# Statistics, routing lists and late weights of an eight-core attention and expert layer in another order

## The reference

```python
x = x + attn(layernorm(x))          # Q = ln @ Wq + bq; K = V = Q
#   probs = softmax(Q @ Q.T / 32);  out = probs @ Q        (2048 x 1024 a core)
x = x + ffn(layernorm(x))
#   scores = sigmoid(h @ gate_w.T);  top 4 of 32 experts by scores + e_bias
#   weights = chosen scores / their sum
#   out = sum over chosen e of  weight_e * (silu(h @ w1[e]) * (h @ w3[e])) @ w2[e]
#   w1, w3: 1024 x 768, w2: 768 x 1024, float32
```

## Time and profile before

| | |
|---|---|
| median of three runs | 1770.35 us (1752.7 to 1800.26) |
| the profiled execution | 1748.2 us; its span 1746.8 us, so 1.4 us lie outside |
| cores in it | 1707.2 to 1746.8 us; the page is of the slowest |
| busy share of the span | PE 72%, PEld 40%, ACT 25%, DVE 23%, POOL 21% |
| granted clock of PE, mean | 0.856 on that core |
| HBM, that core | 349.21 MB read, 52.72 MB written |
| Q phase, attention phase, expert phase | 0 to 124, 124 to 480, 480 to 1747 us |

### The profile page before, as it was taken

How to read it: one execution, slowest core, us unless ns; L and a number is a source line. 1 busy time by engine, 2 the same in 40 slices (tenths; PEclk the granted TensorE clock), 3 DMA queues, 4 the chain that set the end, 5 groups by cost and what they waited for, 6 DMA issues and landing times.

```text
span 1746.8 us, 20430 instructions; the slowest of 8 cores (1707.2 to 1746.8 us)
## 1 busy us (share of the span) xinstructions
PE 1250.8 (72%) x7138; PEld 705.6 (40%) x7209; DVE 399.3 (23%) x874; ACT 431.4 (25%) x613; POOL 367.4 (21%) x359
## 2 busy tenths in 40 slices
PE   4788987999606966666776776667677766677696
PEld 2444543555403533333343443344344433434353
DVE  3433543455501211111111111111111111111121
ACT  3443332333202211112222221122222211222131
POOL 0000011112322222222222222232222222322122
PEclk9889998999757988888888888888888887888898
DMA  9980265421167999999999999999999999999833
GB/s 203 194 167 13 73 62 47 58 78 62 50 71 127 168 169 171 171 169 170 171 169 167 165 166 167 169 167 161 173 169 175 173 167 168 170 164 166 160 70 55
DMA packets 45895, 241.72 MB, mean 138 GB/s; under 512 B 10424, under 2 KB 11064, under 8 KB 33248
## 3 DMA queue, kind: packets, MB, share of 16 engines
q0 software_dynamic: 35136, 209.95, 72.7%
q1 hardware_dynamic: 10512, 30.41, 8.0%
q10 hardware_dynamic: 144, 0.03, 0.0%
HBM read 349.21 MB, written 52.72 MB: 230 GB/s over the span
## 4 chain that ended last, share of the span: by engine, by line
DMA 54%; PE 27%; issue 9%; POOL 3%; DVE 2%; ACT 2%; POOLq 1%; DVEq 0%; SPq 0%; ACTq 0%
DMA out<-yb,t_meta 51%; PE pav L458 7%; PE pss L418 6%; PE pss L767 5%; POOL out L822 3%; PE ptr L296 2%; PE pav L798 2%; PE pss L340 2%; PE ptr L508 2%; DMA xg<-xnd,t_meta 2%; DMA xb<-xd 1%; DVE t_st L246 1%; DVE t_st L247 1%; ACT lnf L317 1%; DVE vq L347 0%
## 5 line engine op out<-in xcount | busy, mean ns | idle before, releaser
L296 PE MATMUL ptr<-c_idb,xg 128*128 128x128 bf16 x768 | 87.2, 297 | 380.4 <-DMA xg<-xnd,t_meta 366.1
L767 PE MATMUL pss<-xgt,wp 128*128 128x384 bf16 x2016 | 339.2, 328 | 1.4 <-ACT xgt L754 1.4
L767 PEld LDWEIGHTS pss<-xgt,wp 128*128 128x128 bf16 x2016 | 198.0, 98 | 135.9 <-issue 4.7
L296 PEld LDWEIGHTS ptr<-c_idb,xg 128*128 128x128 bf16 x768 | 72.9, 135 | 398.2 <-issue 397.8
L781 DVE TENSOR_TENSOR at<-sil,pss 128x384 bf16<-128x384 bf16 x192 | 106.5, 554 | 484.9 <-PE pss L767 484.9
L822 POOL DMA_INDIRECT out<-yb,t_meta x96 | 146.6, 1527 | 307.4 <-DMA out<-yb,t_meta 241.8
L807 DVE TENSOR_SCALAR yb<-pav,t_meta 128x512 f32<-128x512 f32 x96 | 72.1, 751 | 581.7 <-PE pav L798 576.8
L754 ACT COPY xgt<-ptr 128x1024 bf16<-128x1024 bf16 x96 | 97.2, 1012 | 433.5 <-PE ptr L296 353.8
L778 ACT ACTIVATE sil<-pss 128x384 bf16<-128x384 f32 x192 | 94.3, 491 | 358.4 <-PE pss L767 358.4
L767 PE MATMUL pss<-xgt,wr 128*128 128x384 bf16 x1056 | 178.8, 326 | 0.0
L798 PE MATMUL pav<-wp,at 128*128 128x512 bf16 x735 | 174.0, 396 | 4.1 <-issue 3.3
(11 more groups left out here) (100 smaller groups left out, 772.0 us busy)
## 6 DMA issues: line engine op xcount, KB each, us to landing
wp<-w1d POOLq DMA_DIRECT2D x21, 1536.0 KB, 40.6
wp<-w3d POOLq DMA_DIRECT2D x21, 1536.0 KB, 36.2
wp<-w2d POOLq DMA_DIRECT2D x21, 1536.0 KB, 29.5
wr<-w3d POOLq DMA_DIRECT2D x11, 1536.0 KB, 36.8
wr<-w2d POOLq DMA_DIRECT2D x11, 1536.0 KB, 31.1
wr<-w1d POOLq DMA_DIRECT2D x11, 1536.0 KB, 40.9
xb<-xd SPq DMA_DIRECT2D x32, 512.0 KB, 6.4
out<-xb SPq DMA_DIRECT2D x16, 512.0 KB, 3.5
```

The source lines that it names most:

```text
L296: ins = e.transpose(dst[:, k * 128:(k + 1) * 128], src_of(k), ident)
L767: ins = e.matmul(pss[:, bnk * 512:bnk * 512 + CAP], unit_ap(u, c * ID + ic * 128, 128), xgt[:, xo + c * CAP:xo + (c + 1) * CAP], start=(c ...
```

## The change

- The Q phase: `a_stats` only makes statistics; normalizing a tile is `a_ln`, one tile an iteration. The statistics of tiles `j + 3` and `j + 4` stand ahead of the bias add of tile `j` (odd `j`). The loads of x tiles 2 and 3 wait for the two halves of Wq. Of the weight units, one is issued for three tiles instead of one for two, so four in the loop, and the last three wait for the product of tile 12.
- Weights lie in memory in six pieces, each 128 rows x 1024 values (4 KB a row), 512 KB in one piece. A unit's DMA has 768 pieces of 4 KB to read and 2 KB to write where it had 128 of 24 and 12 KB.
- Units 7 to 10: `convert_unit` has POOL's queue round them from memory to memory (`wcd`) at the end of the Q phase and in the first three attention iterations. After attention SP loads the rounded copies, all four, 12 KB a row.
- Routing: tiles 14 and 15 are groups of their own. A record's row is place x 32 + expert, computed in float (the count is scaled by 32 as ACT copies it), neighbouring places 256 bytes apart; the list is read back in three runs of 256 bytes for each partition. Fewer DVE steps (two instructions instead of four in a Newton step; shift and mean folded into one), the mask first, the weights while PE counts; two small products of the combine weights go to POOL. The steps stand at fixed points, no longer 11 at a time.

The core of the diff:

```diff
+CONV = tuple(range(NP_UNITS, RING))
+PIECE = 1024
...
+GROUPS = [(j, j + 1) for j in range(0, NT - 2, 2)] + [(NT - 2,), (NT - 1,)]
...
-    w1d = nc.dram_tensor("w1d", [E, 128, UNIT], F32, kind="ExternalInput").ap()
...
+    w1d = nc.dram_tensor("w1d", [E, NPC, 128, PIECE], F32, kind="ExternalInput").ap()
...
-    mtd = nc.dram_tensor("mtd", [128 * 512, 2], U32, kind="Internal").ap()
+    wcd = nc.dram_tensor("wcd", [len(CONV), 128, UNIT], BF16, kind="Internal").ap()
+    mtd = nc.dram_tensor("mtd", [T * E, 2], U32, kind="Internal").ap()
...
-        for j in range(1, XR):
-            x_tok[j] = load_x(j)
+        x_tok[1] = load_x(1)
         t_bq = p.d(lambda e: e.dma_start(out=bq[:, :], in_=bqd), "dB")
-
-        mtv = mtd.rearrange("(q c) w -> q c w", q=128)
+        for j in range(2, XR):
+            x_tok[j] = load_x(j, t_wq[j - 2])
+
+        mtv = mtd[0:CAP * E, :].rearrange("(b q e) w -> q b (e w)", b=NB, q=128)
...
 
+        def convert_unit(k, *waits):
+
+            e_i, i = divmod(CONV[k], 3)
+            p.d(lambda e: e.dma_start(out=wcd[k, :, :].rearrange("p (c n) -> p c n", n=PIECE),
+                                      in_=wsrc[i][e_i, :, :, :].rearrange("c p n -> p c n")),
+                "dV", *waits, eng="gpsimd")
+
         def load_unit(u, *waits):
+            if u in CONV:
+                k = CONV.index(u)
+                u_tok[u] = p.d(lambda e: e.dma_start(out=unit_ap(u, 0, UNIT), in_=wcd[k, :, :]),
+                               f"dH{k}", p.cnt("dV"), *waits)
+                return
             e_i, i = divmod(u, 3)
-            u_tok[u] = p.d(lambda e: e.dma_start(out=unit_ap(u, 0, UNIT),
-                                                 in_=wsrc[i][e_i, :, :]),
+            u_tok[u] = p.d(lambda e: e.dma_start(
+                out=unit_ap(u, 0, UNIT).rearrange("p (c n) -> p c n", n=PIECE),
+                in_=wsrc[i][e_i, :, :, :].rearrange("c p n -> p c n")),
                            f"dU{u % RING}", *waits, eng="gpsimd")
 
...
             for j in tiles:
-                s = j % XR
-                ln_tok[j] = p.s(lambda e, j=j, s=s: e.activation(
-                    lnf[:, (j % 2) * H:(j % 2 + 1) * H], xb[:, s * H:(s + 1) * H],
-                    AF.Identity, bias=col(C_NMR + j), scale=col(C_RSTD + j)),
-                    v_r, tl_tok.get(j - 2))
-                if j + XR < NT:
-                    x_tok[j + XR] = load_x(j + XR, ln_tok[j])
-                    if j % 2 == 0:
-                        load_unit(j // 2, x_tok[j + XR])
+                st_tok[j] = v_r
+
+        def a_ln(j):
+            s = j % XR
+            ln_tok[j] = p.s(lambda e: e.activation(
+                lnf[:, (j % 2) * H:(j % 2 + 1) * H], xb[:, s * H:(s + 1) * H],
+                AF.Identity, bias=col(C_NMR + j), scale=col(C_RSTD + j)),
+                st_tok[j], tl_tok[j - 2] if j >= 2 else None)
+            if j + XR < NT:
+                x_tok[j + XR] = load_x(j + XR, ln_tok[j])
+                if j % 3 == 0:
+                    load_unit(j // 3, x_tok[j + XR])
 
         def a_tl(j):
...
-        groups = [[0], [1], [2, 3], [4, 5], [6, 7], [8, 9], [10, 11], [12, 13], [14, 15]]
-        ready = 0
-        gi = 0
-        while gi < 2:
-            a_stats(groups[gi])
-            gi += 1
+        for j in (0, 1):
+            a_stats([j])
+            a_ln(j)
         a_tl(0)
         for j in range(NT):
             if j + 1 < NT:
                 a_tl(j + 1)
-            if gi < len(groups) and groups[gi][0] <= j + 2:
-                a_stats(groups[gi])
-                gi += 1
+            if j == 0:
+                a_stats([2, 3])
+                a_ln(2)
+            elif j % 2 == 1 and j + 4 < NT:
+                if j == 1:
+                    a_ln(3)
+                a_stats([j + 3, j + 4])
+                a_ln(j + 3)
+            elif j % 2 == 0 and j + 3 < NT:
+                a_ln(j + 3)
             a_q(j)
             if j >= 1:
                 a_tq(j - 1)
         a_tq(NT - 1)
-        for u in range((NT - XR) // 2, NP_UNITS):
-            load_unit(u, x_tok[NT - 1])
+        for u in range((NT - XR + 2) // 3, NP_UNITS):
+            load_unit(u, q_tok[NT - 4])
+        convert_unit(0, q_tok[NT - 1])
...
+        s_sr = p.s(lambda e: e.activation(c_srep[:, :], pss[:, 0:E], AF.Copy, scale=-1.0), t_sr)
+        p.v(lambda e: e.tensor_scalar(c_eb5[:, :], c_eb[:, :], 0.5, None, ALU.add), tc_all)
...
+        def route_norm(g):
+
+            for j in GROUPS[g]:
+                s = j % XR
+                i = j % 2
+                nst = p.s(lambda e, s=s, i=i, j=j: e.activation(
+                    xn[:, i * H:(i + 1) * H], xb[:, s * H:(s + 1) * H], AF.Identity,
+                    bias=col(C_NMR + j), scale=col(C_RSTD + j)),
+                    rstd_tok[g], nst_tok.get(j - 2), pha_t if j < 2 else None)
+                nst_tok[j] = p.d(lambda e, i=i, j=j: e.dma_start(
+                    out=xnd[j * 128:(j + 1) * 128, :], in_=xn[:, i * H:(i + 1) * H]),
+                    f"dN{i}", nst)
...
-                rt(R_OP, 256).rearrange("p (a e) -> p a e", e=E), AX.X, ALU.add)))
-            work.append(lambda: p.v(lambda e: e.tensor_scalar(
-                a1, ad, 127, 9, ALU.bitwise_and, ALU.logical_shift_left)))
-            work.append(lambda: p.v(lambda e: e.tensor_scalar(
-                a2, ad, 7, 5, ALU.logical_shift_right, ALU.logical_shift_left)))
-            work.append(lambda: p.v(lambda e: e.tensor_tensor(a1, a1, a2, ALU.bitwise_or)))
...
-            def places():
-                v = p.v(lambda e: e.tensor_tensor(
-                    ad.rearrange("p (s k) -> p s k", s=2),
-                    a1.rearrange("p (s k) -> p s k", s=2),
-                    free_ap(idx[:, 0:1], [[8, 2], [1, KTOP]]), ALU.bitwise_or))
-                if g == NT // 2 - 1:
-                    att_t = av_tok[(NT - 1, 1)]
-                    for u in range(NP_UNITS, RING - 2):
-                        load_unit(u, att_t)
...
+            p.v(lambda e: e.tensor_tensor(op, oh, bk(t_pos[:, j0 * E:(j0 + n) * E]), ALU.mult),
+                pe_tok[g])
+            p.v(lambda e: e.tensor_reduce(
+                rt(R_AD, n * KTOP).rearrange("p (a o) -> p a o", o=1), opr, AX.X, ALU.add))
+            v = p.v(lambda e: e.tensor_tensor(
+                t_addr[:, j0 * KTOP:(j0 + n) * KTOP].rearrange("p (s k) -> p s k", s=n),
+                rt(R_AD, n * KTOP).rearrange("p (s k) -> p s k", s=n),
+                free_ap(idx[:, 0:1], [[8, n], [1, KTOP]]), ALU.add))
+            wt_tok[g] = v
+            for i in range(n * KTOP):
+                c = j0 * KTOP + i
+                p.d(lambda e, c=c: e.indirect_dma_start(
+                    out=mtd[:, :],
+                    out_offset=bass.IndirectOffsetOnAxis(ap=t_addr[:, c:c + 1], axis=0),
+                    in_=t_tok[:, 2 * c:2 * c + 2], in_offset=None,
+                    bounds_check=bound(e, T * E - 1), oob_is_err=True),
+                    "dSC", v, t_mi, eng="gpsimd")
+
+            p.v(lambda e: e.tensor_reduce(
...
+        x_free = {}
+        pending = []
...
-        for j in range(NT + 3):
+        for j in range(NT + 2):
+            here = [g for g, tiles in enumerate(GROUPS) if tiles[-1] == j - 2]
...
+            if j + 1 < len(CONV):
+                convert_unit(j + 1, s_tok[(j, 0)])
+            for g in here:
+                router(g)
+                last = g == len(GROUPS) - 1
+                route_choose(g, (lambda g=g: route_norm(g)) if last else (lambda: None))
+                for i in GROUPS[g]:
+                    if i + XR < NT:
+                        xb_load[i + XR] = load_x(i + XR, x_free[i], xj_tok[(i, 1)], ost_tok[i])
...
-            pos_mm()
+            if j == NT:
+                for u in range(NP_UNITS, RING):
+                    load_unit(u, av_tok[(NT - 1, 1)])
+            route_places_mm()
             if j < NT:
                 p_transpose(j)
-            pop_back(11)
-            pos_mm()
-            if 2 <= j < NT + 2 and j % 2 == 0 and j - 1 < NT:
-                back.extend(pair_work((j - 2) // 2))
-        while back:
-            pop_back(1)
-            pos_mm()
+            for g in here:
+                if g == len(GROUPS) - 1:
+                    z_tok.append(p.g(lambda e: e.memset(xg[:, :].bitcast(F32), 0.0),
+                                     av_tok[(NT - 1, 1)]))
+                route_lists(g)
+            for g, tiles in enumerate(GROUPS):
+                if tiles[-1] == j - 1:
+                    route_rstd(g)
+                    if g < len(GROUPS) - 1:
+                        route_norm(g)
 
...
-            out=t_meta[:, :].rearrange("q (c w) -> q c w", w=2), in_=mtv[:, 0:NCOL, :]),
+            out=t_meta[:, :].rearrange("q (b n) -> q b n", b=NB), in_=mtv),
...
         gather(1)
-        for u in range(RING - 2, RING):
```

269 lines of the change are left out of this document (127 added, 142 removed).

## The result

The changed kernel takes 1727.1 us (median of four runs, 1725.6 to 1753.9) beside 1761.5 for the kernel before on the same chip (four runs, 1750.8 to 1800.3): ratio of comparable runs 0.985, 95% interval 0.983 to 0.988. That is 1.5% or 26 us less, where the prediction had 44 (1748.2 to 1704, profiled execution against its like). The time lies in the wide range of 1664 to 1755 and just above the forecast's own, 1690 to 1724. The direction is right, but the change is little more than half of the forecast and within the 2% that a measurement can tell: it fell in the band between 1717 and 1788, which had a chance of 0.27.

A forecast was written before the change was run, and what follows sets the result against it. Bounds: chained waits in the Q phase, waiting for the list before the experts, transfers in the expert phase. 1748.2 - 25 - 31 + 12 = 1704 us; own range 1690 to 1724, wide range 1664 to 1755.

The forecast's parts named there:

- The routing steps: Attention phase: PE sets the pace, so shorter DVE work and moved steps change nothing; 0, within 8 us either way.
- rival 5: More gain: closer records complete sooner and disturb less, pieces cost nothing; attention phase -8, total 1672 us; chance 13%.
- Term A: Q phase: removing the bias add ahead of the statistics ends PE's repeated stalls; -25 us, between -10 and -32.
- rival 1: Q phase: loading of x becomes the pace, leaving a gain of only 10 us; total 1723 us; chance 10%.
- The conversions: Early attention phase: some 15 us each, hidden by the first tiles' scores; 90 us for all seven loads and conversions if unhidden.
- Term B: Way from attention's last product to the first expert: list loaded sooner; -31 us, between -20 and -40.
- Term C: Expert phase: 85 units loaded in 4 KB pieces take 1.5% more transfer time; +12 us.
- Rival 3: Expert phase: the 512 KB step between a row's pieces costs 3%, +25 us; total 1721 us; chance 10%.
- The thought that a memory near its rate: Expert phase: memory is nearly the limit, so the pieces' extra cost would vanish; sum 12 us lower.
- Rival 4: Expert phase: fixed cost per piece or a queue running dry makes it slower, at 20% +167 us, 1863; chance 12%.
- the microsecond named as a sign of being wrong: Expert phase: the prediction is wrong if the expert scatters' period moves over a microsecond either way, 31 us at the end.

The follow-up runs named there:

- e1: Changed kernel with the normalizations of all tile groups moved behind the tanh of their routing, as the last group's already were; ratio to the kernel before 0.962.
- e10: Changed kernel with a pair's normalizations kept in their step but placed behind the x2t copies; no ratio, lowest 1678.6 us, attention 316.4 us.
- e4: Kernel before with its list rows 1 KB apart in place of 4 KB; ratio to the kernel before 0.973.
- e9: e6 with tiles 14 and 15 routed as one pair again; no ratio, lowest 1679.2 us, mean span 1656.0 us.
- e8: e6 without conversions, units 7 to 10 loaded as float32 on GpSimd's queue as before; ratio to the kernel before 0.962, lowest 1664.4 us.
- e6: Changed kernel with the edits of e1 and e2 together: late normalizations and 24 KB weight rows; ratio to the kernel before 0.960.
- e3: Changed kernel with its list rows 4 KB apart again in place of 256 bytes; ratio to the kernel before 1.000.
- e2: Changed kernel with weights in single 24 KB rows again in place of six 4 KB pieces; ratio to the kernel before 0.985.
- e13: e1 with the six pieces of a row 4160 bytes apart in place of 512 KB; ratio to the kernel before 0.963.
- e12: Kernel before with the change's Q phase and list rows 1 KB apart; no ratio, lowest 1671.9 us, mean span 1658.9 us.

## Why the prediction was wrong

**The routing steps: this step failed.** It read: "The clearing of `xg` and the norm's earlier place on ACT could each touch PE by a microsecond a pair: 0, within 8 either way." The place was named, and its price not worked out. PE waits for the copies, the copies queue behind the norms, the norms wait for DVE's root: by the order of the change alone that is a new chain into the engine that sets the pace, and I had no row for the root's end against the copies' start. It is 2.8 us a pair and 13 at tile 14, 28 us on cores 4 to 7 (e1, e10), twice that on cores 0 to 3 and some 41 us of the time. That the wait through the copies is the way it costs is shown by e10; why it costs more on one die is not. Two more things lie under the +14.6 us of the phase. The distance of the lists gives 20 (e4); the prediction had this as part of rival 5, at 8. The rest of the change costs 6 there, 310.8 to 317.0 from e4 to e1, of which 27.7 - 23.0 = 4.7 come behind the last exponentials, where e9 shows the single tile to cost 6. So -20 + 6 + 28 = +14, where 0 stood.

**Term A** was right: -25 between -10 and -32, measured -20.9, and rival 1 (x sets the pace) fell; PE is busy 41.07 of 43 us. **The conversions** were priced rightly at nothing and wrongly in length: their landings took 53.8 and 57.6 us, not 15, but PE was busy 33.35 of 34 us beside two of them, and e8 without them has an attention phase of 315.2 us beside 317.0.

**Term B** had nearly the size, -31 against -36.2, and part of the reasons. The load of the list was to follow the last product by 490 - 462.2 = 27.8 us, and did by 29.3. The four units, whose landing I made the limit, are near it: on cores 2 to 7 the fourth lands 27.4 to 30.5 us behind the last product and the list's load is issued within 0.8 us of that; on core 1 it lands at 21.4, the last record is issued at 22.0, and the load at 24.2. So the units cost up to some 5 us here. e8 doesn't get them back: two float32 units run beside its records in their place and land at 23.6 to 26.6 us on cores 0 to 3. No run has the records alone. By the runs the 36 us are 19 from the distance of the list rows (e4), 15 from the new order of the routing (e4 to e9, which also has the converted units) and 2 to 3 from the single last tile (e9 to e6). The shares depend on the order of the steps: taken out of the finished kernel, the distance is worth 4 us of the way (e3). The prediction had read the earlier trace rows, 0.67 us for a 4 KB packet beside records against 0.207, and used it as a bound for the pieces and, in rival 5, as 8 us; the cause that these rows pointed to was the largest found in the kernel before, 46 us of mean span (e4).

**Term C** had the size, +12, measured 16.8 in the periods less 3.7 in the tail, 13; the steady period moved by 0.6 us, under the microsecond named as a sign of being wrong. Part of that is luck. The 3.7 of the tail were not foreseen and have no explanation, and the profiled execution of before has a period 0.2 us above every other kernel with 24 KB rows, 5 us in 29. Kernels that differ in the pieces give 22.6 less 3.0, 20 (e2), and 29 x 0.56 less 3.8, 12 (e1 to e6). Rival 3 gave the cost to the 512 KB step. The page named there, the Trainium skill's DMA: Bandwidth & Descriptors, Latency and other measured facts, has 207 GB/s against 214, 3%, for copies whose rows lie 512 KB apart from partition to partition, which isn't where the step lies here. e13 without the step costs as much as e1 with it, and the period grew by 1.5 to 2.1% (e1 to e6, e2). The thought that a memory near its rate (the 358 GB/s of the Trainium skill, HBM Reference, Specifications (TRN2)) would swallow the cost of the pieces isn't borne out either: the period follows their number. Rival 4, a fixed cost of each piece, named the mechanism, at 0.6 us an expert or 0.2 a unit, where it needed 0.66 a unit to use up A and B.

Together: A gave 4 us less than forecast, B 5 more, C cost 1 more, the step at 0 cost 15, and 1 lies before the fourth scatter. These leave -28 on cores 4 to 7, where the prediction had -44. In the time it is -26: the slowest core is among 0 to 3, which lose more in attention.

## What to carry to other kernels

When a change moves an instruction ahead of others on an engine in order, price it by what it waits for, not by its own length: take the end of its last input from the trace and ask who waits for what then stands behind it. Here two norms of 1.3 us a pair ahead of the copies cost 28 us of the phase on the better cores and some 41 us of the time, and moved a few instructions on they were free.

When all engines stand still at once and the DMA share is near 1 at almost no bytes, look at where small scattered writes go before anything is reordered. One shift constant in the kernel before gave 2.7%, and with the Q phase's part (e12) the mean span is within 11 us of the best kernel here, without the pieces, the split, the conversions or the new routing. That holds for a standstill with a full DMA share; the one on core 3 of the changed kernel has an empty one, and its cause is open.

A layout that cuts long rows in pieces must buy something elsewhere. Here it bought nothing: e6 has everything else with rows of 24 KB, and its mean span is 14 us under e1.
